# Attention loop of a graph network: target one-hot on ScalarE, another load order, the MLP's first layer behind the k product

## The reference

```python
q = (x @ Wq).reshape(n, H, DQK)                     # 8 heads of 16
x_dst = x[edge_dst]
wk = relu(e @ k_w1 + k_b1) @ k_w2 + k_b2            # e: 64 edge features
wv = relu(e @ v_w1 + v_b1) @ v_w2 + v_b2
k = (sum over s of sh[:, s] * (x_dst @ Cqk[:, s])) * wk      # s = 0..8
v = (sum over s of sh[:, s] * (x_dst @ Cv[:, s])) * wv
attn = sum over d of q[edge_src] * k                # per head
ex = exp(attn - segment_max(attn)[edge_src])
upd = segment_sum(v * ex / segment_sum(ex))
out = batchnorm(x @ W_self + upd @ W_out)
```

## Time and profile before

| | us |
|---|---|
| median of 3 runs | 5155.87 |
| range of the runs | 5151.41 to 5162.44 |
| profiled execution | 5154.97 |
| its span, first to last instruction | 5153.2 |
| TensorE busy | 4427.7 |
| VectorE busy | 4161.0 |
| ScalarE busy | 2259.1 |

### The profile page before, as it was taken

How to read it: one execution, slowest core, us unless ns; L and a number is a source line. 1 busy time by engine, 2 the same in 40 slices (tenths; PEclk the granted TensorE clock), 3 DMA queues, 4 the chain that set the end, 5 groups by cost and what they waited for, 6 DMA issues and landing times. The chain is left out here.

```text
span 5153.2 us, 91855 instructions
## 1 busy us (share of the span) xinstructions
PE 4427.7 (86%) x21874; PEld 3147.8 (61%) x21874; DVE 4161.0 (81%) x9462; ACT 2259.1 (44%) x4914; POOL 2409.1 (47%) x2660
## 2 busy tenths in 40 slices
PE   1788877879999999999999999999998677777777
PEld 0222343557777777777777777777777566666665
DVE  5999956479999999999999999999996455555554
ACT  0777740045555555555555555555553100000000
POOL 1000000045555555555555555555552377777774
PEclk7999978789999999999999999999998555555555
DMA  2121116377777777777777777777773244444442
GB/s 56 75 92 83 75 50 262 122 170 175 176 176 175 177 176 175 174 176 175 176 174 174 175 175 176 174 175 176 174 175 78 63 102 103 103 103 102 103 102 64
DMA packets 576584, 719.34 MB, mean 140 GB/s; under 512 B 204519, under 2 KB 338727, under 8 KB 572583
## 3 DMA queue, kind: packets, MB, share of 16 engines
q1 hardware_dynamic: 517910, 634.65, 49.1%
q0 software_dynamic: 52288, 81.11, 7.3%
q10 hardware_dynamic: 6288, 2.48, 0.2%
HBM read 663.58 MB, written 54.36 MB: 139 GB/s over the span
## 5 line engine op out<-in xcount | busy, mean ns | idle before, releaser
L1328 POOL DMA_INDIRECT attn_rows<-x_twice,attn_idx x808 | 988.4, 1223 | 237.6 <-issue 198.3
L1684 POOL DMA_INDIRECT msg_rows<-a_rows,msg_idx x808 | 778.9, 964 | 370.3 <-issue 241.2
L1271 ACT CAST attn_z_hi<-attn_z 128x512 fp32r<-128x512 f32 x1010 | 621.9, 620 | 184.9 <-DVE attn_z L1526 155.1
L1526 DVE TENSOR_TENSOR attn_z<-attn_xt,attn_sh 128x512 f32<-128x512 f32 x1010 | 679.0, 689 | 27.1 <-ACT attn_xt L1259 6.1
L1347 POOL TENSOR_TENSOR acc_den<-acc_den,attn_sums 128x256 f32 x808 | 582.0, 720 | 188.7 <-POOL acc_den L1347 151.9
L1722 PE MATMUL msg_at_dst<-msg_bwin,msg_pick 128*128 128x64 f32 x1616 | 397.7, 428 | 270.8 <-DVE msg_pick L1748 193.3
L1722 PEld LDWEIGHTS msg_at_dst<-msg_bwin,msg_pick 128*128 128x128 f32 x1616 | 359.9, 328 | 351.1 <-DVE msg_pick L1748 227.9
L1532 DVE TENSOR_TENSOR attn_z_lo<-attn_z,attn_z_hi 128x512 fp32r<-128x512 f32 x808 | 551.2, 682 | 0.8 <-ACT attn_z_hi L1271 0.7
L1662 ACT ACTIVATE msg_msg<-msg_pre 128x256 f32<-128x256 f32 x202 | 84.1, 417 | 941.5 <-DVE msg_pre L1763 937.1
L1349 POOL MEMSET acc_den<- 128x6656 f32 x1 | 5.6, 5646 | 978.6 <-POOLq L90 978.6
L538 PE MATMUL count_bank<-count_key_hot,count_lo_hot 128*128 128x400 bf16 x1395 | 328.7, 346 | 137.8 <-DVE count_key_hot L496 134.5
(11 more groups left out here) (293 smaller groups left out, 10927.0 us busy)
## 6 DMA issues: line engine op xcount, KB each, us to landing
attn_sh<-in_edge_sh SPq DMA_DIRECT2D x404, 640.0 KB
attn_dst<-dst_scaled SPq DMA_DIRECT2D x202, 256.0 KB
attn_qwin<-q_rows SPq DMA_DIRECT2D x808, 64.0 KB
attn_mask<-dst_step SPq DMA_DIRECT2D x202, 256.0 KB, 3.4
msg_dst<-dst_scaled SPq DMA_DIRECT2D x202, 256.0 KB, 3.2
counts<-chunk SPq DMA_DIRECT2D x15, 3100.0 KB, 9.7
chunk_late<-counts SPq DMA_DIRECT2D x15, 3100.0 KB, 10.4
attn_feat<-in_edge_feat SPq DMA_DIRECT2D x404, 64.0 KB
```

Of the source, the lines that this page charges most:

```text
L1271: nc.scalar.copy(z_hi[p][:, c, :], z[:, c % 2, :]).then_inc(high_sb, 1)
L1328: pool.indirect_dma_start(rows[p][:, t, :], None, dram["x_twice"], bass.IndirectOffsetOnAxis(ap=idx[p][:, t:t + 1], axis=0)).then_inc(rows ...
L1526: dve.tensor_tensor(z[:, c % 2, :], xt[p][:], sh[p][:, c, :], ALU.mult).then_inc(z_ready, 1)
L1684: pool.indirect_dma_start(rows[p][:, t, :], None, dram["a_rows"], bass.IndirectOffsetOnAxis(ap=idx[p][:, t:t + 1], axis=0)).then_inc(rows_ ...
```

## The change

Six edits. The one-hot is made by ScalarE: four Abs of (target - column) and one Relu of (1 - that), in `body` after `et` and before `take_rows`; it is made in its own group's round and held in two buffers. VectorE's one-hot is dropped. `pick` gets two buffers, and `make_pick` moves ahead of `maxima`. TensorE's first layer moves out of `prepare` into `hidden`, between k product and second layer, and its second half is written to `b_attn` instead of `b_v`, with the waits that this asks for. ScalarE's `hidden` moves behind `high(..., 2)`. SyncE issues a group's targets first.

```diff
@@ -1166,8 +1166,8 @@
             ph.sem(n) for n in ("pick_ready", "z_ready", "low_ready", "ran", "topped", "shifted", "onehot_ready",
                                 "kw_ready", "u_ready", "vw_ready", "dve_set"))
 
-        xt_sb, hid_sb, w_sb, ex_sb, vt_sb, sum_sb, high_sb = (
-            ph.sem(n) for n in ("xt_sb", "hid_sb", "w_sb", "ex_sb", "vt_sb", "sum_sb", "high_sb"))
+        xt_sb, hid_sb, w_sb, ex_sb, vt_sb, sum_sb, high_sb, apart = (
+            ph.sem(n) for n in ("xt_sb", "hid_sb", "w_sb", "ex_sb", "vt_sb", "sum_sb", "high_sb", "apart"))
 
         vx_ready = ph.sem("vx_ready")
         added, acc_clear = ph.sem("added"), ph.sem("acc_clear")
@@ -1188,8 +1188,8 @@
         hid = [ph.sb(f"hid{p}", [P, GE]) for p in two]
         wk = ph.sb("wk", [P, GE])
         wv = ph.sb("wv", [P, GE])
-        pick = ph.sb("pick", [P, TG, P])
-        onehot = ph.sb("onehot", [P, TG, P])
+        pick = [ph.sb(f"pick{p}", [P, TG, P]) for p in two]
+        onehot = [ph.sb(f"onehot{p}", [P, TG, P]) for p in two]
         u = ph.sb("u", [P, GE])
         vw = [ph.sb(f"vw{p}", [P, GE]) for p in two]
         vx = ph.sb("vx", [P, GE])
@@ -1259,9 +1259,20 @@
                 nc.scalar.copy(xt[p][:], b_xt[:]).then_inc(xt_sb, 1)
                 stage_idx(g + 2, p)
 
+            def make_onehot(g, p):
+
+                if not (is_first(g, 0) or is_first(g, 1)):
+                    act.wait_ge(sum_ps, g - 1)
+                for t in range(TG):
+                    nc.scalar.activation(onehot[p][:, t, :], sb["iota_row"][:], ACT.Abs, scale=-1.0,
+                                         bias=sb["dst_local"][:, bass.ds(TG * g + t, 1)]).then_inc(apart, 1)
+                act.wait_ge(apart, TG * (g + 1))
+                nc.scalar.activation(onehot[p][:], onehot[p][:], ACT.Relu, scale=-1.0, bias=sb["ones"][:, 0:1]
+                                     ).then_inc(onehot_ready, 1)
+
             def hidden(g, p):
                 act.wait_ge(hid_ps, g + 1)
-                for half, bank in enumerate((b_hid_vt, b_v)):
+                for half, bank in enumerate((b_hid_vt, b_attn)):
                     nc.scalar.activation(hid[p][:, half * (GE // 2):(half + 1) * (GE // 2)], bank[:, 0:GE // 2], ACT.Relu,
                                          bias=sb["L2_b1"][:, 0:1]).then_inc(hid_sb, 1)
 
@@ -1278,8 +1289,8 @@
                 if not (is_first(g, 0) or is_first(g, 1)):
                     empty_den(p)
                 if next:
+                    high(g + 1, q, 2)
                     hidden(g + 1, q)
-                    high(g + 1, q, 2)
                 if front:
                     act.wait_ge(w_ps, g + 1)
                     if not is_first(g, 0):
@@ -1294,6 +1305,8 @@
                     act.wait_ge(vt_ps, g)
                     nc.scalar.copy(vt[:], b_hid_vt[:].rearrange("p (t c) -> p t c", t=TG)).then_inc(vt_sb, 1)
                     nc.scalar.copy(et[:], b_wv_den[:].rearrange("p (t c) -> p t c", t=TG)).then_inc(vt_sb, 1)
+                if front:
+                    make_onehot(g, p)
                 if has_two(g):
                     take_rows(*in_two(g, n, p))
                 if back:
@@ -1370,6 +1383,10 @@
             def load(g, n, p, first):
                 edges = bass.ds(g * GE, GE)
                 if not first:
+                    sp.wait_ge(pick_ready, g - 1)
+                sp.dma_start(dst[p][:], dram["dst_scaled"][bass.ds(g * GE, GE)].partition_broadcast(P)
+                             ).then_inc(dst_in[p], 16)
+                if not first:
                     sp.wait_ge(hid_ps, g - 1)
                 for half in two:
                     sp.dma_start(feat[p][half * D:(half + 1) * D, :],
@@ -1381,10 +1398,6 @@
                     sp.dma_start(sh[p][k * D:(k + 1) * D, :, :], dram["edge_sh"][k::2, edges].partition_broadcast(D)
                                  ).then_inc(sh_in[p], 16)
                 if not first:
-                    sp.wait_ge(pick_ready, g - 1)
-                sp.dma_start(dst[p][:], dram["dst_scaled"][bass.ds(g * GE, GE)].partition_broadcast(P)
-                             ).then_inc(dst_in[p], 16)
-                if not first:
                     sp.wait_ge(q_ps, g - 1)
                 for t in range(TG):
                     sp.dma_start(qwin[p][:, t, :], dram["q_rows"][bass.ds(bases[t], P), :]).then_inc(qwin_in[p], 16)
@@ -1409,20 +1422,22 @@
                 for t in range(TG):
                     mm = nc.tensor.transpose(b_xt[:, t * P:(t + 1) * P], rows[p][:, t, :], sb["ident"][:])
                 mm.then_inc(xt_ps, 1)
+
+            def hidden(g, n, p):
                 pe.wait_ge(feat_in[p], 32 * (n + 1))
                 if not is_first(g, 0):
                     pe.wait_ge(hid_sb, 2 * g)
                 if not (is_first(g, 0) or is_first(g, 1)):
-                    pe.wait_ge(vw_ready, g - 1)
+                    pe.wait_ge(shifted, 2 * (g - 1))
                 nc.tensor.matmul(b_hid_vt[:, 0:GE // 2], sb["L2_w1"][0:D, :], feat[p][0:D, :], start=True, stop=True)
-                nc.tensor.matmul(b_v[:, 0:GE // 2], sb["L2_w1"][D:P, :], feat[p][D:P, :], start=True,
+                nc.tensor.matmul(b_attn[:, 0:GE // 2], sb["L2_w1"][D:P, :], feat[p][D:P, :], start=True,
                                  stop=True).then_inc(hid_ps, 1)
 
             def pick_q(g, n, p):
                 pe.wait_ge(qwin_in[p], 64 * (n + 1))
                 pe.wait_ge(pick_ready, g + 1)
                 for t in range(TG):
-                    mm = nc.tensor.matmul(b_q[:, t * P:(t + 1) * P], qwin[p][:, t, :], pick[:, t, :],
+                    mm = nc.tensor.matmul(b_q[:, t * P:(t + 1) * P], qwin[p][:, t, :], pick[p][:, t, :],
                                           start=True, stop=True)
                 mm.then_inc(q_ps, 1)
 
@@ -1446,6 +1461,9 @@
                     prepare(*after(g, n, p))
                 if front:
                     split_product(b_k, "L2_Cqk", g, p, True).then_inc(k_ps, 1)
+                if next:
+                    hidden(*after(g, n, p))
+                if front:
                     pe.wait_ge(hid_sb, 2 * (g + 1))
                     if is_first(g, 1):
                         pe.wait_ge(w_sb, 2)
@@ -1457,8 +1475,6 @@
                                      stop=True).then_inc(w_ps, 1)
                     if back:
                         pe.wait_ge(vw_ready, g)
-                    if next:
-                        pe.wait_ge(hid_sb, 2 * (g + 2))
                     split_product(b_v, "L2_Cv", g, p, False).then_inc(v_ps, 1)
                 if back:
                     pe.wait_ge(vx_ready, g)
@@ -1466,6 +1482,8 @@
                         pe.wait_ge(w_sb, 2 * (g + 1))
                     else:
                         pe.wait_ge(sum_sb, 2 * (g - 1))
+                    if next:
+                        pe.wait_ge(hid_sb, 2 * (g + 2) - 1)
                     for t in range(TG):
                         nc.tensor.transpose(b_hid_vt[:, t * P:(t + 1) * P], vx[:, t * P:(t + 1) * P], sb["ident"][:])
                     for t in range(TG):
@@ -1474,6 +1492,8 @@
                     mm.then_inc(vt_ps, 1)
                 if front:
                     pe.wait_ge(u_ready, g + 1)
+                    if next:
+                        pe.wait_ge(hid_sb, 2 * (g + 2))
                     nc.tensor.matmul(b_attn[:], sb["head_sum"][:], u[:], start=True, stop=True).then_inc(attn_ps, 1)
                 if next:
                     pick_q(*after(g, n, p))
@@ -1481,15 +1501,16 @@
                     pe.wait_ge(vt_sb, 2 * g)
                     pe.wait_ge(onehot_ready, g)
                     for t in range(TG):
-                        nc.tensor.matmul(b_wk_sum[:, t * P:(t + 1) * P], vt[:, t, :], onehot[:, t, :],
+                        nc.tensor.matmul(b_wk_sum[:, t * P:(t + 1) * P], vt[:, t, :], onehot[q][:, t, :],
                                          start=True, stop=True)
                     for t in range(TG):
-                        mm = nc.tensor.matmul(b_wv_den[:, t * P:(t + 1) * P], et[:, t, :], onehot[:, t, :],
+                        mm = nc.tensor.matmul(b_wv_den[:, t * P:(t + 1) * P], et[:, t, :], onehot[q][:, t, :],
                                               start=True, stop=True)
                     mm.then_inc(sum_ps, 1)
 
             def first(g, n, p):
                 prepare(g, n, p)
+                hidden(g, n, p)
                 pick_q(g, n, p)
 
             run_rounds(pe, first, body)
@@ -1508,9 +1529,9 @@
 
             def make_pick(g, n, p):
                 dve.wait_ge(dst_in[p], 16 * (n + 1))
-                if not is_first(g, 0):
-                    dve.wait_ge(q_ps, g)
-                dve.tensor_tensor(pick[:], dst[p][:].rearrange("p (t e) -> p t e", t=TG),
+                if not (is_first(g, 0) or is_first(g, 1)):
+                    dve.wait_ge(q_ps, g - 1)
+                dve.tensor_tensor(pick[p][:], dst[p][:].rearrange("p (t e) -> p t e", t=TG),
```

(13 more changed lines are left out.)

## The result

The changed kernel takes **5075.42 us** (median of 4 runs, 5073.11 to 5084.4), the kernel before 5153.64 beside it (4 runs, 5149.4 to 5162.44): a ratio of 0.9847, 95% interval 0.9834 to 0.9861. The forecast was 5073. Some lines have other numbers in the new kernel: the forward scan is now L1583, the pick L1534, z L1547, the second u L1609, the rows' transposes L1423 and the one-hot L1267 and L1270.

The account below looks back on a forecast made before the run. VectorE was taken as the bound, then the chain over xt's copy: 13.76 us plus 0.04 for disturbances makes 13.80 against 14.21 a round; 0.41 x 201 = 82 us, 5155 - 82 = 5073 us, own range 5053 to 5103, stated range 5027 to 5122.

Parts of the forecast that it names:

- (1): On VectorE: the one-hot leaves, the pick takes its place at its cost; 0.60 us saved, own round 13.61 us.
- (2): Closed chain z, splits, u, head_sum, rows' transposes, xt's copy, z: only 0.37 of 0.60 us gained, round 13.76 us.
- rival A: VectorE alone is the bound: round 13.61 us, time 5034 us; chance 0.13.
- (3): On ScalarE: four Abs and one Relu take 1.9 us, fit the 3.56 us hole before xt's copy, cost nothing.
- (4): On TensorE: first layer moved behind the k product saves 0.1 to 0.4 us of TensorE, worth nothing in time.
- The second chain: Transposes, k product, second layer, wk on ScalarE, z_hi 3, z_lo 3 on VectorE: slack 0.05 to 0.1 us.
- (5): First layer, head_sum and vx's transposes get new waits through hid's halves and b_attn: all cost nothing.
- (6): SyncE's queue issues the same bytes in another order, dst earlier, sh one transfer later: 0 us.

Follow-up runs that it names:

- the cut adds: Changed kernel with GpSimd's adds cut to the first column of each 128-wide window: 5715.22 us against 5452.32, ratio 1.0515.
- The last run: Changed kernel with GpSimd's gather ahead of its adds and the rows' transposes ahead of the sums, exponential at its old place: 5030.33 us, ratio 0.9757.

## Why the prediction was right

**(1) One-hot off VectorE, pick in its place: right.** The pick's median rose from 684 to 841 ns, as the one-hot's row had said. The run with the pick back confirms that the place matters, and the cut adds show why the place is dear. VectorE's own round came out at 13.61 once the chain was out of the way; in that run no wait of VectorE in the loop sums to more than 3.0 us over 184 rounds.

**(2) xt's copy is late next: right, 0.06 us short.** The chain is 13.82 us, not 13.76, because z starts 0.12 us after the end of ScalarE's copy (2514.40 to 2514.52), where I had carried over the 0.05 read between VectorE and TensorE. The sum had 13.80, with 0.04 added for small disturbances; the mean over the loop is 13.85. I expected 0.2 us a round of idle VectorE with xt's copy as releaser; the brackets give 0.14 (26.3 / 184), the distance to the small instruction 0.23. The last run shows by experiment that the chain, and not VectorE alone (rival A), was the bound: with the chain shortened the kernel runs at A's round and at A's time, 5030 against 5034 (on another chip; the kernel before takes 5156.4 there). Against the run with the gather first, 13.82 us a round, the transposes' place is all that differs.

**(3) One-hot on ScalarE: right.** From 2510.16 to 2512.20, 2.04 us, against 1.9 estimated and 2.2 as the upper bound; four of 128x128 take 1.28 us together. The hole is down to 1.6 us as forecast, and the two fill runs show that it has an edge: two activations more cost nothing, four cost 1.14 us a round. By the rule of the Trainium skill ("ScalarE: Activation LUTs", "Rules for kernel authors") the one-hot should have stayed on VectorE. As a price it holds, 2.04 us there against 0.80 in the earlier trace rows; as advice it did not hold here, since the measured hole costs nothing and VectorE was the bound.

**(4) First layer moved: worth nothing in time, right; one number behind it wrong.** I forecast that TensorE's wait for u would fall to 0.2 us. It is 0.36, and 0.20 with the layer back in its old place, so the difference belongs to the move. The step that failed is TensorE's own round, left at 13.74. The second layer now starts 4.28 us after the transposes (2513.17 to 2517.45) instead of 4.58: the 0.30 lies inside the 0.1 to 0.4 that I had named for the two switches between 64-row and 128-row work and had then not carried on. With 13.44 the wait comes to 13.82 - 13.44 = 0.38. That the switches are the cause fits the Trainium skill ("TensorEngine Tiling (Array Packing)", section "Tiling Modes"), by which a change of tiling mode drains the engine; no run isolates them from the move itself. The second chain came out as worked out: the cast of z_hi 3 ends 5.70 us after z 0 (forecast 5.72), z_lo 3 starts at 5.79 (forecast 5.82). The 0.09 between them is about a hand-over, so no slack is left; but nothing was lost, since z_lo 3 starts 5.82 us after z 0 on the mean of the rounds, and 5.83 before the change.

**(5) New waits: right,** and even the wait that the new bank avoids, 0.73 us before the v product, would have cost nothing.

**(6) Targets first: right number, thin reason, and so in part luck.** I took 0, because no bracket on VectorE named a transfer. That held for the change as made. But the row showed only that a load was in time for a pick at 2535.58, not for one 4.2 us earlier. Undone, this part costs 2.1 us a round. The prediction should have listed "the targets land too late for the earlier pick" as a rival, and given the reason for its small chance: this part of the diff.

The total of 5073 against 5075.42 rests on the terms (1) and (2). The chain is measured 0.06 us from its forecast, VectorE's own round to 0.01. That the totals agree to 2 us is partly luck: the forecast gain was 82 us, all of it in the rounds, and the rounds of the profiled executions gave 72, 0.36 us each instead of 0.41; where the other 6 of the 78 between the medians come from, the traces don't tell.

## What to carry to other kernels

When a piece of work leaves the bounding engine, ask what its slot had covered: here the slot in front of a scan had to stay filled, and only the swap with the pick made a gain. An instruction that moves earlier needs its input loaded earlier, and a load's absence from the list of waits says nothing about the new place. When a closed chain is next, look at what feeds the link to be moved: here the producer (the gather) had to go ahead before the consumer (the transposes) could; the consumer alone made it slower, and both together gave a further 0.9% (0.9757 against 0.9847, each to the kernel before on its own chip).

## What the runs showed of the hardware

- Adds of 128x256 on GpSimd beside VectorE lengthen a 128x512 comparison from 682 to 841 ns at the median and a backward scan from 1225 to 1286 (up to 1432); with adds of 128x2 both are at their short form.
- z on VectorE starts 0.12 us after the end of ScalarE's copy; TensorE's matmul started 0.06 us after VectorE's u (2509.47 to 2509.53).
- The wait in VectorE's bracket counts from the end of the instruction before. As the next can start 0.08 us before that end, a bracket is 0.08 us short and small waits have none: 0.14 us a round in the brackets, 0.23 in truth.
- The idle time in a matmul's bracket understated what TensorE could spare: 0.36 us there, and a wait of 0.73 us elsewhere in the round cost nothing.
- Less work on one engine made the kernel slower (cut adds, 5%), because the signal of TensorE's transposes reached ScalarE 3.17 us after their last start instead of 0.28, in half of the rounds; why, the records don't show.
